# A four-layer convolution kernel on one core: weights of two frequencies in one transfer, sides of the mixing product swapped, and the odd-phase planes split first at the image turn

## What is computed

```
x = x + conv3x3(sign(gn(x)), ternary weights) * alpha
x = x + irfft2(einsum('bchw,cohw->bohw', rfft2(gn(x))[:, :, :56, :57], w))   # w complex, its own 64x64 matrix per frequency
x = x + conv7x7(gn(x)) + bias                                               # written by FFT, a plain 7x7 convolution
x = x + window_attention(gn(x))     # windows of 8x8, q and k cubed and renormalised, depthwise 5x5 on v, projection
```

## Time and profile before

| what | value |
|---|---|
| median of three runs | 11767.94 us (11765.45 to 11776.15) |
| the profiled execution | 11769.75 us, span 11767.7 us |
| part a / part b / preparation / images | about 0 to 1598 / 1598 to 2638 / 2638 to 2783 / 2783 to 11768 us |
| PE busy | 10317.4 us (88%), mean granted clock 0.934 |
| DVE / ACT / POOL busy | 67% / 51% / 33% |
| moved by DMA | 947.34 MB in 1001966 packets |

### The profile page before, as it was taken

How to read it: one execution, slowest core, us unless ns; L and a number is a source line. 1 busy time by engine, 2 the same in 40 slices (tenths; PEclk the granted TensorE clock), 3 DMA queues, 4 the chain that set the end, 5 groups by cost and what they waited for, 6 DMA issues and landing times.

```text
span 11767.7 us, 292004 instructions
## 1 busy us (share of the span) xinstructions
PE 10317.4 (88%) x120871; PEld 9151.4 (78%) x120871; DVE 7890.7 (67%) x13708; ACT 5969.8 (51%) x7016; POOL 3941.8 (33%) x3304
## 2 busy tenths in 40 slices
PE   7989978874999889999999999999889999999996
PEld 5777777774888878888888888888778888888885
DVE  7777722115677777777777777777677777777775
ACT  4666621112555555555555555555555555555553
POOL 0000000002444444444444444444444444444442
PEclk9999988886999999999999999999999999999996
DMA  8999999982111121111111111111121111111100
GB/s 206 239 241 241 245 210 233 235 214 53 28 39 36 44 45 36 36 37 37 39 36 39 36 39 37 39 39 36 42 46 37 36 36 38 36 39 38 37 22 17
DMA packets 1001966, 947.34 MB, mean 81 GB/s; under 512 B 592800, under 2 KB 937872, under 8 KB 980944
## 3 DMA queue, kind: packets, MB, share of 16 engines
q1 hardware_dynamic: 972048, 708.59, 28.4%
q0 software_dynamic: 28608, 220.21, 5.0%
HBM read 605.77 MB, written 322.96 MB: 79 GB/s over the span
## 4 chain that ended last, share of the span: by engine, by line
PE 38%; DVE 17%; ACT 7%; issue 7%; POOL 5%; DMA 1%; SPq 0%; DVEq 0%; POOLq 0%; ACTq 0%
PE c_ps L1029 24%; PE c_ps L1100 3%; POOL c_cube L1740 3%; PE c_ps L1178 3%; PE c_ps L1113 2%; PE c_ps L1165 2%; DVE c_v L1542 2%; ACT c_xp L1286 2%; DVE c_xp L1506 2%; DVE c_bn L1486 2%; DVE c_s L1605 2%; DVE c_xr L1524 2%; ACT c_sq L1349 1%; ACT c_xp L1226 1%; DVE c_qt L1580 1%
## 5 line engine op out<-in xcount | busy, mean ns | idle before, releaser
L1029 PE MATMUL c_ps<-c_xp,c_wst 128*128 128x224 f16 x45696 | 4911.4, 265 | 154.8 <-DVE c_xp L1506 154.8
L1029 PEld LDWEIGHTS c_ps<-c_xp,c_wst 128*128 128x128 f16 x45696 | 4366.7, 98 | 634.9 <-issue 415.6
L1715 POOL TENSOR_TENSOR c_xr<-c_sm,c_xr 128x448 f32<-128x448 f32 x448 | 704.0, 1572 | 2217.0 <-DVE c_xr L1524 2216.9
L1740 POOL TENSOR_TENSOR c_cube<-c_sq,c_qk 128x896 f32<-128x896 f32 x448 | 928.3, 2093 | 1194.3 <-ACT c_sq L1340 1194.3
L1317 ACT ACTIVATE c_qt<-c_ps 128x896 f32<-128x896 f32 x224 | 205.8, 919 | 2042.1 <-PE c_ps L1121 2042.1
L1275 ACT ACTIVATE c_tn<-c_xr,c_nrm 64x448 f32<-64x448 f32 (+1 forms) x832 | 956.0, 1153 | 57.0 <-DVE c_xp L1506 27.0
L1100 PE MATMUL c_ps<-c_wqkv,c_xn 64*128 64x192 f32 x6272 | 791.2, 367 | 200.5 <-DVE c_v L1542 193.0
L619 PE MATMUL b_ps<-b_xs,b_wt 64*64 64x64 f32 x6384 | 774.2, 294 | 207.0 <-DVE b_xj L595 160.8
L1286 ACT ACTIVATE c_xp<-c_tn 128x1080 f16<-128x1080 f32 (+1 forms) x544 | 572.2, 1063 | 737.4 <-DVE c_tn L1499 733.6
L1506 DVE TENSOR_TENSOR c_xp<-c_tn,c_xp 128x1080 f16<-128x1080 f32 (+1 forms) x544 | 664.1, 1230 | 271.7 <-ACT c_xp L1286 270.7
L1100 PEld LDWEIGHTS c_ps<-c_wqkv,c_xn 64*128 64x128 f32 x6272 | 516.3, 195 | 384.5 <-DVE c_v L1542 287.2
(11 more groups left out here) (158 smaller groups left out, 17750.2 us busy)
## 6 DMA issues: line engine op xcount, KB each, us to landing
b_wt<-in_L_conv_weight SPq DMA_DIRECT2D x56, 2048.0 KB, 21.8
a_xc<-in_x SPq DMA_DIRECT2D x64, 1568.0 KB, 21.4
x<-a_x1s POOLq DMA_DIRECT2D x64, 1568.0 KB, 12.1
a_xh<-x SPq DMA_DIRECT2D x64, 1568.0 KB
c_xr<-x SPq DMA_DIRECT2D x224, 448.0 KB, 4.0
out<-c_xr SPq DMA_DIRECT2D x448, 224.0 KB, 3.1
b_xs<-xf SPq DMA_DIRECT2D x28, 2048.0 KB, 24.5
yf<-b_ys POOLq DMA_DIRECT2D x28, 2048.0 KB, 12.1
```

What stands on the lines that cost most here:

```text
L1029: ins = pe.matmul(sums(c, p), wst[:, ws, pr, FIRST_TAP[p] + k].rearrange("p q o -> p (q o)"), xp[:, xs, PLANE[kind] + f, row:row + CROWS, ...
L1715: pool.tensor_tensor(here, apart(sm[:, half]).unsqueeze(1).to_broadcast([P, 2, CROWS, QW]), here, ALU.add).then_inc(s.added, 1)
L1740: pool.tensor_tensor(cube[:, :, k].rearrange("p q r c -> p r q c"), sq[:, :, :, k], qk[:, :, :, k], ALU.mult).then_inc(done, 1)
```

## The change

**Part b.** The pairs are formed otherwise: pair 2m+u holds the frequencies 4m+u and 4m+2+u (the constant `fwd_h` is permuted for that). One weight transfer for each half now brings the weights of two bodies (4096 KB, contiguous runs of 1024 bytes instead of 512); `wt` holds two such steps. xs has one buffer, and the load of body k waits for the turn of body k-1. The turn writes `xt` with three parts (-imaginary, real, imaginary), the images side by side. The product takes the data as the stationary side (64 contiguous numbers) and the weights as the moving side (64 numbers, 1024 bytes apart). The result has part and image on the partitions and output channel and column in the free dimension. `ys` has one buffer, and each store is four transfers of 32 partitions; a body's copies wait for the whole store of the body before. yf is laid out by image, so that `load_ys` reads 56 partitions of 16 KB each, twice. PE's loop holds four bodies.

**Preparation.** The 14 high parts go to ACT. Of the 8 spread matrices DVE builds 5 and POOL 3 (a product and a sum for each term).

**Turn of the image.** `tn` has three buffers instead of two. For the chunks 0 to 2 the o planes are differenced, rounded and split first, with signals of their own, the other six planes after them. PE starts the convolution when the o planes of the chunks 0 and 1 are there, does products 0 to 2 first (72 matmuls), and the others wait for all planes of chunk 2. FIRST_PIECES changes with it.

```diff
+    kh = k.reshape(KP // 2, 2, 2).transpose(0, 2, 1).reshape(-1)     # order of rows in fwd_h
-        wt = sb("wt", [P, 2, C, FP // 2, 2])
-        xs = sb("xs", [P, 2, B, FP // 2, 2])
-        xj = sb("xj", [P, 2, B, FP // 2, 2])
-        ys = sb("ys", [P, 2, B, FP // 2, 2])
+        wt = sb("wt", [P, 2, C, 2, FP // 2, 2])
+        xs = sb("xs", [P, B, FP // 2, 2])
+        xt = sb("xt", [P, 2, KW, 3, B])
+        ys = sb("ys", [P, C, FP // 2])
...
+            def load_x(k):
+                if above_zero(k):
+                    sp.wait_ge(turned, k)
+                sp.dma_start(xs[:], xf[bass.ds(k, 1)]...).then_inc(x_loaded, 16)
+            load_w(0, 0)
+            load_x(0)
+            load_w(1, 1)
+            for k in range(1, 4):
+                load_x(k)
+            with sp.Fori(0, KP // 4 - 1) as t:
+                for odd in range(2):
+                    load_w(2 * t + (2 + odd), odd)
+                    for u in range(2):
+                        load_x(4 * t + (4 + 2 * odd + u))
...
-                pool.dma_start(yf[bass.ds(k, 1)].rearrange("k p b f -> (k p) (b f)"), ys[:, odd])
+                for half in range(2):
+                    for r in range(2):
+                        rows = slice(C * half + B * r, C * half + B * r + B)
+                        there = yf[:, r, bass.ds(4 * m + (2 * half + u), 1)]
+                        pool.dma_start(there.rearrange("b k o w -> (b k) (o w)"), ys[rows]...)
...
-                dve.tensor_scalar(xj[:, odd, :, 0:KW, 0], xs[:, odd, :, 0:KW, 1], -1.0, None, ALU.mult)
-                dve.tensor_copy(xj[:, odd, :, 0:KW, 1], xs[:, odd, :, 0:KW, 0]).then_inc(turned, 1)
+                by_freq = xs[:, :, 0:KW].rearrange("p b w r -> p r w b")
+                dve.tensor_scalar(xt[:, odd, :, 0], by_freq[:, 1], -1.0, None, ALU.mult)
+                dve.tensor_copy(xt[:, odd, :, 1], by_freq[:, 0])
+                dve.tensor_copy(xt[:, odd, :, 2], by_freq[:, 1]).then_inc(turned, 1)
...
-                                ins = pe.matmul(ps[rows, 4 * half + g % 4, at:at + 2 * B], wt[rows, odd, :, f, r],
-                                                src[rows, odd, :, f], ...)
+                                ins = pe.matmul(ps[C * half:C * half + 2 * B, 4 * half + g % 4, at:at + C],
+                                                xt[rows, u, f, 1 - r:3 - r].rearrange("p r b -> p (r b)"),
+                                                wt[rows, odd, :, u, f, r], ...)
...
+            for t in range(25):                      # prepare_weights, POOL; SPREAD_DVE = 5
+                pool.tensor_tensor(here, taps[:, t]..., stencil[:, SPREAD_DVE:WS, t]..., ALU.mult)
+                    pool.tensor_tensor(there, term[:], there, ALU.add)
+            for ky in range(7):                      # prepare_weights, ACT
+                for q in range(2):
+                    ins = act.activation(place(0, ky, q), turned_taps(ky), ACT.Copy)
...
-FIRST_PIECES = (0, 40, 0, 64, 0, 150, 188)
+FIRST_PIECES = (0, 72, 0, 96, 0, 150, 188)
-        ys = sb("ys", [P, C, FP])
+        ys = sb("ys", [P, C, FP // 2])
-        tn = sb("tn", [P, 2, SLOTS, ROWS, PW])
+        tn = sb("tn", [P, TNS, SLOTS, ROWS, PW])     # TNS = 3
...
-                high_part(n, 0)                      # ACT, after padded_chunk 0 and 1
-                high_part(n, 1)
+                odd_high(n, 0)
                 padded_chunk(n, odd, 2)
+                odd_high(n, 1)
+                rest_high(n, 0)
+                odd_high(n, 2)
+                rest_high(n, 1)
                 padded_chunk(n, odd, 3)
-                high_part(n, 2)
+                rest_high(n, 2)
                 high_part(n, 3)
...
-                qkv(0); differ 0; differ 1; low 0; padded_low 2; low 1; padded_low 3; qkv(1); differ 2; low 2; qkv(2); differ 3; low 3; qkv(3); relu
+                qkv(0); odd_low 0; differ 0; odd_low 1; rest_low 0; differ 1; odd_low 2; rest_low 1; qkv(1); differ 2; rest_low 2; padded_low 3; differ 3; low 3; qkv(2); qkv(3); relu
```

More of the change, by code:

```diff
@@ L541, in _, with store @@
             pool.memset(ys[:], 0.0).then_inc(padded, 1)
[L543 removed]
+            def store(m, u):
+                k = 2 * m + u
                 for half in range(2):
@@ L623, in body, with step @@
                                     ins.then_inc(mixed[half], 1)
-            body(0, 0)
-            body(1, 1)
-            with pe.Fori(1, KP // 2) as t:
+            def step(t):
                 for odd in range(2):
-                    body(2 * t + odd, odd)
+                    for u in range(2):
+                        body(2 * t + odd, odd, u)
+            step(0)
+            with pe.Fori(1, KP // 4) as t:
+                step(t)
 TOK = WS * WS
@@ L652 @@
 ORDER = [(p, i) for p in range(NP) for i in range(12 * PRODUCTS[p][2])]
-FIRST_ORDER = sorted(ORDER, key=lambda o: o[0] < NP - 1 and o[1] >= 3 * PRODUCTS[o[0]][2] or 2 * (o[0] == NP - 1))
+FIRST_ORDER = sorted(ORDER, key=lambda o: 2 if o[0] >= 3 else o[1] >= 3 * PRODUCTS[o[0]][2])
 NB, NT = HALVES, NP - HALVES
 EARLY = 4
+TNS = 3
+O_FIRST = 3
 COPIED = (1, 4, 7, 10)
@@ L687, in prepare_weights, with turned_taps, place @@
         soft_done, scaled_up, split, reordered = sem("soft_done"), sem("scaled_up"), sem("split"), sem("reordered")
+        pool_at, high_put = sem("pool_at"), sem("high_put")
+        def turned_taps(ky):
+            return ps[0:C, 3 * (ky % 2):3 * (ky % 2) + 3].rearrange("c b x -> c (b x)")[:, 0:TAPS * C].rearrange(
+                "c (k o) -> c k o", k=TAPS)
+        def place(part, ky, q):
+            pr, rp = divmod(ky + q, 2)
+            return to["wst"][C * rp:C * rp + C, part, pr, :, q]
         LOADS = [
@@ L717, in _ @@
             pool.memset(to["wst"][:], 0.0).then_inc(cleared, 1)
+            pool.wait_ge(loaded, 16 * len(LOADS))
+            pool.nop(nofuse=True)
+            shape = [P, WS - SPREAD_DVE, P]
+            for t in range(25):
+                there = to["spread"][:, SPREAD_DVE:WS]
+                here = there if t == 0 else term[:]
+                pool.tensor_tensor(here, taps[:, t].unsqueeze(1).to_broadcast(shape),
+                                   stencil[:, SPREAD_DVE:WS, t].unsqueeze(2).to_broadcast(shape), ALU.mult).then_inc(pool_at, 1)
+                if t:
+                    pool.wait_ge(pool_at, 2 * t)
+                    pool.nop(nofuse=True)
+                    pool.tensor_tensor(there, term[:], there, ALU.add).then_inc(pool_at, 1)
+                pool.wait_ge(pool_at, 2 * t + 1)
+                pool.nop(nofuse=True)
         @block.scalar
@@ L803, in _ @@
             for ky in range(7):
-                dve.wait_ge(turned, ky + 2)
-                got = ps[0:C, 3 * (ky % 2):3 * (ky % 2) + 3].rearrange("c b x -> c (b x)")[:, 0:TAPS * C].rearrange(
-                    "c (k o) -> c k o", k=TAPS)
+                dve.wait_ge(high_put, ky + 1)
                 for q in range(2):
-                    pr, rp = divmod(ky + q, 2)
-                    high = to["wst"][C * rp:C * rp + C, 0, pr, :, q]
-                    dve.tensor_copy(high, got).then_inc(dve_at, 1)
-                    dve.wait_ge(dve_at, done.next())
-                    ins = dve.tensor_tensor(to["wst"][C * rp:C * rp + C, 1, pr, :, q], got, high, ALU.subtract)
+                    ins = dve.tensor_tensor(place(1, ky, q), turned_taps(ky), place(0, ky, q), ALU.subtract)
                 ins.then_inc(split, 1)
             for t in range(25):
-                for d in range(WS):
+                for d in range(SPREAD_DVE):
                     if t == 0:
@@ L925, in ring, with planes_get, planes_put @@
             return places
+        def planes_get(k, odd):
+            lo, hi = spans[k]
+            there = tn[:, k % TNS, 0:9, 0:hi - lo].rearrange("p (g q) j w -> p g q (j w)", g=3)
+            return there[:, 1] if odd else there[:, 0:3:2]
+        def planes_put(part, k, odd):
+            (at, rows), = ring(k)
+            there = xp[:, part, :, at:at + rows].rearrange("p (g q) j w -> p g q (j w)", g=3)
+            return there[:, 1] if odd else there[:, 0:3:2]
         def pad_put(k):
-            return tn[:, k % 2, PLANE["o"] + 1:SLOTS:X0_AT - PLANE["o"] - 1, :, 1:1 + QW]
+            return tn[:, k % TNS, PLANE["o"] + 1:SLOTS:X0_AT - PLANE["o"] - 1, :, 1:1 + QW]
         def pad_get(odd):
```

191 lines of the change are left out of this document (113 added, 78 removed).

## The result

The changed kernel takes 11734.19 us (median of 10 runs, 11718.45 to 11746.94), the kernel before, run beside it, 11764.05 (11752.25 to 11776.5). The ratio is 0.9973, with a 95% interval of 0.9965 to 0.9982: 30 us faster. The forecast was 11,771, no change. The profiled execution of the changed kernel spans 11716.8 us, 17 less than its median; that of before, 11767.7, lies at its median. So the two traces differ by 51 us and the medians by 30, and stage by stage the traces are read first for where the time went.

A forecast was written before the change was run, and what follows sets the result against it. PE was taken to bound nearly everything except part b, bound by its transfer chain, and the preparation. Terms 44 - 20 - 2 - 12 - 6 - 3 = +1 gave 11769.75 + 1 = 11,771 us, no change; range 11,650 to 11,905.

The forecast's parts named there:

- 44 - 20 - 2 - 12 - 6 - 3 = +1: Whole kernel: part b, preparation, memsets, first ys load, 31 image turns and first image, in us, together +1.
- Part b, +44: Part b: a pass chain of 73.4 us against 72.3, with longer ends, 1082 us against 1038, so +44 us.
- Matmuls, "a body stays at 28.8 us": Part b on PE: cheaper weight loads offset by strided reading on the moving side, a body unchanged at 28.8 us.
- Rival D: Part b on PE: the moving side reads each number twice, 57.6 us a body, total 12,390; chance 5%.
- preparation: Preparation: casts leave DVE's chain (-11), 75 spread operations leave DVE (-21), slowing with POOL 12: -20 us.
- First load: Before PE's first image matmul: smaller ys load -12 us, memsets -2 us.
- First image: First image's turn, with no attention behind it: -3 us.
- Turn: Image turn: convolution starts 2.8 us earlier, mostly returned as longer waits; 0.2 us gained for 31 turns, -6 us.
- A: Part b: stores and weight loads collide fully, 10.2 us a store, a pass 83.8 us, total about 11,905; chance 17%.
- B: Part b: stores hide beside the weights, a pass of 60 to 66 us, total 11,620; chance 14%.
- C: Image turn: it pays in full, 2.7 us x 31 = -84 us, total 11,690; chance 13%.
- E: Part b weight transfers: longer runs lift the rate to 220 GB/s, a pass 2.8 us shorter, total 11,731; chance 6%.

The follow-up runs named there:

- b_shift: Kernel before plus 115 waits on an already set semaphore ahead of PE's image stage, moving its loop start to the changed kernel's place: 11736.12 us, ratio 0.9976.
- a_unshift: Changed kernel plus 143 such waits ahead of PE's image stage, moving its loop start back: 11751.7 us, ratio to before 0.9987.
- a_end: Changed kernel plus 160 such waits, so that the instruction block ends after one numerator matmul: 11760.44 us, ratio to before 0.9996.
- b_partb_n: Kernel before with only the new mixing stage (part b) and new yf layout, no added waits: 11746.8 us.
- a_noturn: Changed kernel with the image turn of the kernel before, loop start kept at the changed kernel's place: 11731.01 us, ratio to before 0.9964.
- a_pool_x: Changed kernel with part b's turn at the head of each body and its image data loaded on POOL's queue: 11631.33 us, ratio to before 0.9893.
- b_partb: Kernel before with only the new mixing stage and yf layout, plus 143 waits holding PE's image loop at its old place: 11798.02 us, 6 runs.
- b_partb_r: Second measurement of the kernel before with only the new mixing stage and yf layout plus 143 waits: 11790.94 us, 11 runs.
- a_noturn_u: Changed kernel with the old image turn and 143 waits ahead of PE's image stage, giving a second stop: 11746.73 us.

## Why the prediction was wrong, point by point

**The step that failed** is the sum, "44 - 20 - 2 - 12 - 6 - 3 = +1": it takes the image loop outside its turns as unchanged. A term is missing, the place of the image loop's start in its block of PE's instructions. It measured -31 us in the kernel before (b_shift), and -17.5 and -26 in the kernel after (against a_unshift and a_end), -14 and -21 without the waits' own time: from half of the 30 us to all of them. In the two traces it is the -36.4 of the last rows. The prediction had such a stop in its hands, the 3.8 us after the loop's jump in part b, called a wait for nothing that the trace names. In the trace it lies 27 matmuls behind the jump, in 12 passes, 45 us in all. It was not asked what it is, nor what sets it when the program gets longer.

The other terms come to +1 in the forecast and to -2 in the chain of runs with one stop, and that is in part luck: +11 where they give 44 - 12 - 2 = +30, -16 for -20, and +3 for -6 - 3.

**Part b, +44**: +33.1 in the trace. The chain is right: weights at 206 GB/s, landing at 1870.4 behind 41 us of weights, a pass of 72.3 against 73.4. In it the turn took 5.2 us instead of 6.4 and a store some 4.5 instead of 5. The first matmul came 28 us later, not 20. Measured in runs, with the first ys and at one place of the loop (b_partb_n against b_shift), the edit costs +11 us where the terms give 44 - 12 - 2 = +30; the profiles of the two have +34.7 for the stage and -17.7 for the first ys.

**Matmuls, "a body stays at 28.8 us"**: wrong, to the good. ACT's copies, the measure of a group in the earlier trace rows, now follow one another at 3.56 us:

```profile
1859.22 1.03 ACT L600 ACTIVATE b_ys<-b_ps 64x512 f32<-64x512 f32 x1 [4.80 <-PE b_ps L638]
...
1862.78 1.03 ACT L600 ACTIVATE b_ys<-b_ps 64x512 f32<-64x512 f32 x1 [2.53 <-PE b_ps L638]
```

A body's matmuls take 26 us, but no pass got shorter, as PE waits for data and, in 55 stops, for instructions. Rival D is out: it asks for 57.6 us. A matmul starts every 56 ns, in stretches at a granted clock of 0.50 (1840 to 1843.5) as at 1.00 (1808 to 1816), so something other than the array's clock sets this pace; a small cost of the single numbers on the moving side could hide under it. The rule of the Trainium skill (SBUF — State Buffer, Door 1: The DMA port swizzle) that an access to a new line pays would have it slower; no such cost shows in these rows.

**The other terms**: preparation -17.2 and -18 for -20. First load -15.6 for -14. First image -2.9 for -3, but 3.4 came back in its convolution. Turn: the convolution started 5.85 us after the statistics (6 forecast), and the 2.9 us came back as waits of 1.99 us before L1166 and 1.60 before L1223; L1244 comes 37.1 us behind the statistics on the mean of the 30 turns, instead of 37.4. The reasoning held; a_noturn puts the worth of the new turn at zero.

**Rivals.** A is out: a pass took 72.3 us, not 83.8, and a store cost the weights some 4.5 us, though one more store cost 7.4. B is out for this order of the queue; a_pool_x comes near its time, by another order and not by stores that cost nothing. C is out: it asks for -84 us, and a_noturn measured 3 the other way. E is out: 206 GB/s, not 220; that its time was 11,731 is luck. The Trainium skill's rule on small descriptors (DMA: Bandwidth & Descriptors, Why small descriptors are slow) gave 8% for the longer run by my estimate; the windows give 0.5%.

**What stays open.** Why the second stop costs 44 to 51 us with the new mixing stage alone, and 16 to 31 elsewhere (40 to 47 and 12 to 31 without the waits' own time), though the 15 last rows differ by 30 to 38 us in all these pairs. Part of the spread is a choice in the first row of windows: it takes 32.7 to 33.0 us or 34.3 to 34.5, and the long ones come with a fall of the clock after L1178. Two profiles of the same kernel, b_partb and b_partb_r, have 24 and 10 long ones of 30. In a_noturn and a_noturn_u it is 20 and 5, some 25 us, which pay back most of the 37.5 that the second stop adds to the last rows; in before and b_shift, where the whole 31 us show, it is 14 and 15. A window of before in such a row, and the same place in a short one:

```profile
3612.50:3620.50 8.00, 7.94 (x113) 6.73 (x117) 4.77 (x8) 5.90 (x5) 5.64 (x5) 0.57 0.01 2
```

```profile
3886.50:3894.50 8.00, 6.69 (x150) 5.83 (x148) 6.47 (x14) 5.98 (x5) 5.72 (x6) 1.00 0.02 4
```

What makes the clock fall in one image and not in the next, with the same instructions, no run here shows.

## What to carry to other kernels

A stop marked "issue" behind a loop's jump belongs in the ledger like any transfer: look in which block of 256 instructions the loop starts, how much work the rest of that block holds, and what an edit further up does to it. Compare a change with a version that has the same place before its gain is put down to what it was made for. And where a small transfer queues behind a large one and feeds a chain, try it in another queue before its buffers are changed.

## What the runs showed of the hardware

- Behind a jump of its loop PE stopped for 2.0 to 3.5 us with the DMA engines at rest (share 0.02 to 0.04), and for 1.4 to 3.1 more where 26, ten or one matmul of the block was left (26.5 us in 13 passes of before, 34.9 in a_end). The last rows of these passes got 30 to 38 us longer by it.
- PE also stops in straight code while large transfers run. In part b of after it is 105 us in 56 stops by the profile; one of them, 14.2 us, ends with the second body's turn and is a wait for data, the other 55 are 91 us, mostly 1 to 3 each. Before, it is 55 us in 25 stops, of which 12 behind the loop's jump take 45, so straight code cost 10. There a block's matmuls last longer (64 ns each, not 57).
- A weight load of contiguous numbers took 169 ns in part b instead of 219, and the matmuls 57 ns each (730.48 us for 12768) instead of 64, at either granted clock, with the moving side read number by number.
- Four stores of 32 partitions each, issued together, ran at 216 GB/s alone, the one store over 128 partitions at 437; beside a load into 64 partitions both kinds took some 4.5 us from that load.
- Reading with a stride of 512 bytes, DVE took 1.74 us for 1824 numbers instead of 1.15 (1759 ns against 1147 in the groups of lines).
